# Mixture-of-experts tiles of two half tiles with an expert each, in a fused attention and expert layer

## The chip, the cores and the metric

The kernel runs on one core of a Trainium2 chip. A core has a matrix engine (PE, with its weight loads listed as PEld), a vector engine (DVE), a scalar engine (ACT), a general engine (POOL) and a queue processor (SP) that only issues transfers. Each works off its own list of instructions in order, and they wait for each other by semaphores. The metric is the device time of one execution in microseconds (us).

## The reference

For 128 sequences of 64 tokens with 128 features, the reference first adds a gated cross-attention and then a gated mixture of experts:

```
x = x + tanh(g_xattn) * xattn(ctx, layernorm(x))        # 8 heads, keys from ctx and x
n = layernorm(x)
probs = softmax(n @ Wr + br);  top 2 of 8 experts
h = relu(n @ W1[e] + b1[e])                              # 128 -> 256
y = h @ W2[e] + b2[e]                                    # 256 -> 128
x = x + tanh(g_ffn) * sum over the 2 chosen of probs[e] * y
```

All of it is in 32-bit floats. The reference computes every expert for every token; the kernel computes only the two that are chosen.

## The kernel before

The work is cut into 16 groups of 8 sequences (512 tokens). One program written out by hand runs over slots n from -15 to 179. A slot holds the attention of one sequence in three stages (scores, softmax one slot later, output two slots later) and, by n modulo 8, one of the group's jobs: turning keys, queries, projection, residual, layernorm, routing. Every engine walks through the same slots, so the slots set the order of all queues.

The experts work on chunks of 2, 3, 3, 3, 3 and 2 groups. When a chunk's last group is routed, each token's normalised row has been scattered by POOL to a buffer in HBM that is sorted by expert (`scatter_rows`, L482). `list_tiles` (DVE) then finds which 256-row tiles of that buffer are filled, and writes a table with the first row and the expert of each. The number of tiles of a chunk is a constant, the most that any routing can need: 15, 19, 19, 19, 19, 15, together 106. A tile belongs to a single expert.

`tile_slots` gives each tile a slot: none before its chunk is routed, none in slots with n modulo 8 equal to 2 until slot 136. Slots 35 to 127 hold the 72 tiles of chunks 0 to 3, beside the attention of later groups. The attention ends with slot 130; slots 131 to 164 hold the other 34 tiles (called the tail here), one after the other.

For tile i in slot n:

- SP loads the rows into `xt` four slots ahead (L404), from an address that it read from the table.
- In slot n - 1 PE transposes them (`turn_tile`, L988), ACT copies the result to `xtT` (L618), and the weights and biases of the tile's expert, 642 columns, are copied from `wall` to `wt`: by POOL for the first 72 tiles (L516), by ACT in the tail (L643), both in `fetch_weights`.
- In slot n PE makes the hidden layer (`hidden_tile`, L1004), and DVE adds the bias and clips at zero (L906).
- In slot n + 1 PE makes the output (`output_tile`, L1013), with the weights as the moving operand; DVE adds the bias (L934), SP stores it (L412).

Expert numbers and row numbers are data, so they go through registers: `values_load_multi_w_load_instructions` loads up to eight of them from the table in one instruction, and checks the bounds of each with two more. POOL and ACT do that for the expert (L512, L639), SP for the row (L400), once for 8 tiles.

When a chunk's outputs are stored, POOL gathers them for each group (`gather_rows`, L495, eight indirect transfers per group), DVE adds them to the residual (`combine`, L880 and L885), and SP writes the result. In the attention PE multiplies scores (L1024), transposes the probabilities (L1032) and multiplies them with the values (L1041); the queries (L945 to L947) and the projection (L1072) are jobs of a group.

Of the kernel before, what the change touches and what calls it, by code (L numbers as in the profile page):

```python
# [32 lines left out]
TILE = 256  # L33
J = ROWS // TILE

TILES = tuple((2 * c * TOK + E * (TILE - 1)) // TILE for c in CHUNKS)
# [6 lines left out]
PACK = 2 * D + 2 * D + 2 + D  # L43
# [18 lines left out]
AT_ONCE = 8  # L62
# [68 lines left out]
def flamingo(nc, x, ctx_in, g_xattn, g_ffn, gamma_m, beta_m, gamma_l, beta_l, Wq, bq, Wkv, bkv, Wo, bo,  # L131
# [5 lines left out]
    with ctx:  # L137
# [100 lines left out]
        wt = sb("wt", [P, WB, PACK])  # L238
        hs = sb("hs", [P, 2, 2, TILE])
# [72 lines left out]
        got_x = [sem(f"got_x{b}") for b in range(XB)]  # L312
        wt_early = sem("wt_early")
# [34 lines left out]
        def wait_tiles_read(eng, k):  # L348

            for b in range(XB):  # L350
                wait(eng, got_x[b], 16 * len(range(b, FIRST_TILE[k + 1], XB)))
# [16 lines left out]
        def _(sp):  # L368
            def weights(n):
# [11 lines left out]
                if n == 0:  # L381
                    sp.dma_start(wall[:, :, 0:2 * D], W1.rearrange("e d n -> d e n")).then_inc(got_experts, 16)
                    for c in range(2):
                        sp.dma_start(wall[:, :, (2 + c) * D:(3 + c) * D], W2[:, c * D:(c + 1) * D, :].rearrange("e p n -> p e n")).then_inc(got_experts, 16)
                        sp.dma_start(wall[:, :, 4 * D + c], b1[:, c * D:(c + 1) * D].rearrange("e p -> p e"),  # L385
                                     allow_slow_non_contiguous=True).then_inc(got_experts, 16)
                    sp.dma_start(wall[:, :, 4 * D + 2:PACK], b2.partition_broadcast(P)).then_inc(got_experts, 16)
# [3 lines left out]
            def load_tile(i):  # L391
# [5 lines left out]
                if t % AT_ONCE == 0:  # L397
                    first_rows.clear()
                    m = min(AT_ONCE, TILES[k] - t)
                    _, got = nc.values_load_multi_w_load_instructions(table[0:1, k, t:t + m], engines=(mybir.EngineType.SP,),  # L400
                                                                      min_val=0, max_val=E * ROWS - TILE)
                    first_rows.update(zip(range(i, i + m), got))
                wait(sp, xt_ready, i - XB + 1)
                sp.dma_start(xt[:, i % XB, :, :], xs[k % SETS][bass.ds(first_rows[i], TILE), :].rearrange("(a p) d -> p a d", a=2)).then_inc(got_x[i % XB], 16)  # L404
# [37 lines left out]
        def _(pool):  # L442
# [21 lines left out]
            nc.gpsimd.iota(begins[:, 0, :, :], [[ROWS, E], [TILE, J]], base=0, channel_multiplier=0,  # L464
# [36 lines left out]
            def fetch_weights(i):  # L501
# [3 lines left out]
                if i == 0:  # L505
                    pool.wait_ge(got_experts, 16 * 6)
                if t == 0:
                    wait_shared(pool, shared_out, "table", LAST_GROUP[k], 0)
                if t % AT_ONCE == 0:
                    experts.clear()  # L510
# [617 lines left out]
```

## Time and profile before

| | us |
|---|---|
| median of 3 runs | 954.1 (952.58 to 955.68) |
| the profiled execution, its own time | 955.86 |
| its span, first to last instruction | 953.8 |
| PE busy, of the span | 808.2 (85%) |
| DVE, ACT, POOL busy | 601.6, 514.6, 491.2 |
| attention ends, tail of tiles begins | about 808.7 |
| last tile's output written by DVE | 924.8 |

How to read it: a busy PE is one with a matrix multiplication in flight; a record holds the way through the array too, so busy times overlap and the distance between the starts of two records says more than their length. A 32-bit multiplication is two records. The names of engines with a q (SPq) are their instruction processors.

### The profile page before, as it was taken

Reading aid. Unit: us, or ns where it says so; the run is one execution under the profiler, and the core shown is the slowest. Engines: PE = TensorE matmul, PEld = TensorE weight load, DVE = VectorE, ACT = ScalarE, POOL = GpSimd, SP = SyncE. Lnnn points to the kernel's source line nnn. Section 1 sums busy time; section 2 is a strip of 40 time slices with the busy share of each in tenths; the row PEclk is TensorE's granted clock in tenths of the full one; section 3 lists DMA queues with packets and bytes.
Section 4 is the critical chain, followed back from the end, with each engine's and each line's share of the span. In section 5 each row is a group of like instructions: output and inputs, shape, how many; then the busy total and the mean of one; then the engine's idle time right before and its main releaser. Section 6 shows DMA issues by size and latency. Waiting matters only on the chain.

```text
span 953.8 us, 15888 instructions
## 1 busy us (share of the span) xinstructions
PE 808.2 (85%) x4481; PEld 605.4 (63%) x4481; DVE 601.6 (63%) x1908; ACT 514.6 (54%) x1655; POOL 491.2 (52%) x510
## 2 busy tenths in 40 slices
PE   4747888788999898999899999899999898777760
PEld 4534556464878674878686778677777764656650
DVE  3515475755767756878767677959686754655461
ACT  3537657475757375757475757566666553323320
POOL 2103235252636355766363676657675656572645
PEclk9979999999999999999999999999999999879995
DMA  4953233102121112232212132313131213344532
GB/s 129 372 167 144 86 130 117 50 29 56 53 78 58 52 40 78 64 95 70 74 50 73 51 95 73 89 45 106 51 90 58 81 51 94 96 126 128 139 113 63
DMA packets 113976, 86.14 MB, mean 90 GB/s; under 512 B 11985, under 2 KB 104418, under 8 KB 113890
## 3 DMA queue, kind: packets, MB, share of 16 engines
q1 hardware_dynamic: 99618, 49.32, 18.8%
q0 software_dynamic: 8192, 16.79, 6.0%
q10 hardware_dynamic: 6080, 19.02, 5.0%
q8 instruction: 37, 0.61, 0.3%
q14 instruction: 49, 0.40, 0.1%
HBM read 39.74 MB, written 45.35 MB: 89 GB/s over the span
## 4 chain that ended last, share of the span: by engine, by line
PE 69%; DVE 10%; ACT 7%; issue 5%; SPq 4%; DMA 2%; POOL 2%; POOLq 0%; ACTq 0%; DVEq 0%
PE shared L1072 12%; PE batch L1041 12%; PE batch L1024 9%; PE y_ps L1013 8%; PE hid_ps L1004 8%; PE batch L1032 4%; ACT probs L592 3%; PE shared L947 3%; PE shared L945 3%; PE shared L946 3%; PE xt_ps L988 2%; ACT pT_sb L600 2%; DVE hs L906 2%; SPq L385 2%; PE batch L1004 2%
## 5 line engine op out<-in xcount | busy, mean ns | idle before, releaser
L537 POOL TENSOR_TENSOR probs<-probs,rsums 128x512 f32<-128x512 f32 x128 | 134.6, 1051 | 291.1 <-DVE rsums L900 289.9
L612 ACT ACTIVATE oT<-batch 128x512 f32<-128x512 f32 x128 | 76.5, 598 | 209.0 <-PE shared L1072 114.5
L592 ACT ACTIVATE probs<-batch,neg_max 128x128 f32<-128x128 f32 x512 | 180.4, 374 | 11.8 <-DVE neg_max L894 11.8
L894 DVE TENSOR_REDUCE neg_max<-batch 128x4 f32<-128x512 f32 x128 | 88.0, 687 | 118.8 <-PE batch L1024 117.5
L1041 PE MATMUL batch<-pT_sb,kvn 128*128 128x512 f32 x256 | 140.5, 631 | 24.3 <-ACT pT_sb L600 24.0
L495 POOL DMA_INDIRECT yg<-sorted_y,home x128 | 126.3, 987 | 64.8 <-issue 32.6
L1024 PE MATMUL batch<-kvT,qT 128*128 128x128 f32 x1024 | 141.7, 282 | 17.4 <-ACT oT L612 17.4
L1024 PEld LDWEIGHTS batch<-kvT,qT 128*128 128x128 f32 x1024 | 129.2, 193 | 41.9 <-ACT oT L612 28.7
L482 POOL DMA_INDIRECT sorted_x<-xn,row_of x128 | 130.6, 1020 | 32.5 <-issue 32.0
L1013 PEld LDWEIGHTS y_ps<-wt,hs 128*128 128x128 f32 x848 | 110.1, 196 | 19.1 <-issue 16.3
L1013 PE MATMUL y_ps<-wt,hs 128*128 128x128 f32 x848 | 116.3, 281 | 5.9 <-DVE y_sb L934 5.9
L1072 PE MATMUL shared<-oT,M 128*128 128x512 f32 x256 | 119.3, 610 | 0.8 <-ACT oT L612 0.8
L592 ACT ACTIVATION_READ_ACCUMULATOR probs<-batch,neg_max 128x1 f32 x512 | 110.1, 215 | 0.0
L655 ACT ACTIVATE qT<-shared,tb 128x512 f32<-128x512 f32 x128 | 87.8, 688 | 30.2 <-PE shared L947 26.5
L1004 PE MATMUL hid_ps<-xtT,wt 128*128 128x256 f32 x356 | 94.2, 388 | 8.8 <-issue 8.7
L600 ACT ACTIVATE pT_sb<-batch 128x512 f32<-128x512 f32 x128 | 77.9, 609 | 37.7 <-PE batch L1032 36.3
L906 DVE TENSOR_SCALAR hs<-hid_ps,wt 128x256 f32<-128x256 f32 x178 | 77.1, 474 | 33.5 <-PE hid_ps L1004 33.3
L934 DVE TENSOR_TENSOR y_sb<-y_ps,wt 128x256 f32<-128x256 f32 x106 | 44.3, 418 | 79.3 <-PE y_ps L1013 75.4
L1032 PE MATMUL batch<-ident,probs 128*128 128x128 f32 x512 | 79.6, 279 | 13.3 <-POOL probs L537 13.3
L1072 PEld LDWEIGHTS shared<-oT,M 128*128 128x128 f32 x256 | 48.5, 199 | 51.3 <-issue 51.3
L618 ACT ACTIVATE xtT<-xt_ps 128x256 f32<-128x256 f32 x106 | 40.3, 380 | 63.6 <-PE xt_ps L988 63.6
L1004 PEld LDWEIGHTS hid_ps<-xtT,wt 128*128 128x128 f32 x356 | 61.8, 194 | 16.3 <-issue 11.5
(132 smaller groups left out, 1226.4 us busy)
## 6 DMA issues: line engine op xcount, KB each, us to landing
sorted_x<-yg ACTq DMA_DIRECT2D x36, 512.0 KB, 3.6
xt<-sorted_x SPq DMA_DIRECT2D x106, 128.0 KB
sorted_y<-y_sb SPq DMA_DIRECT2D x106, 128.0 KB
kv<-in_ctx_dram SPq DMA_DIRECT2D x16, 256.0 KB, 3.8
kv<-in_x_dram SPq DMA_DIRECT2D x16, 256.0 KB, 4.3
xres<-in_x_dram SPq DMA_DIRECT2D x16, 256.0 KB, 3.0
out_dram<-x SPq DMA_DIRECT2D x16, 256.0 KB
sorted_x<-xn,row_of POOLq DMA_INDIRECT x128, 2.3
```

The costliest lines, as they stand in the source:

```text
L482: nc.gpsimd.indirect_dma_start(xs[k % SETS][:, :], bass.IndirectOffsetOnAxis(ap=row_of[:, g, choice, c:c + 1], axis=0), xn[:, g % 2, c, :] ...
L495: nc.gpsimd.indirect_dma_start(yg[:, g % 2, c, choice, :], None, ys[k % SETS][0:TILES[k] * TILE, :], bass.IndirectOffsetOnAxis(ap=home[:, ...
L537: nc.gpsimd.tensor_tensor(pv, pv, rsums[:, m % 2, :].unsqueeze(2).broadcast_to([P, 4, P]), ALU.mult).then_inc(probs_ready, 1)
L592: last = nc.scalar.activation(probs[:, m % 2, c * P:(c + 1) * P], batch_ps[m % 3][:, c * P:(c + 1) * P], ACT.Exp, bias=neg_max[:, m % 2, c ...
L600: nc.scalar.activation(pT_sb[:, :], batch_ps[m % 3][:, :], ACT.Copy).then_inc(pT_done, 1)
L906: last = nc.vector.tensor_scalar(hs[:, i % 2, c, :], hid(i)[:, c * TILE:(c + 1) * TILE], wt[:, i % WB, 4 * D + c:4 * D + c + 1], 0.0, ALU. ...
L1004: last = nc.tensor.matmul(hid(i)[:, c * TILE:(c + 1) * TILE], wt[:, i % WB, c * D:(c + 1) * D], xtT[:, i % 2, :], start=True, stop=True)
L1013: last = nc.tensor.matmul(y_ps[:, a * D:(a + 1) * D], hs[:, i % 2, c, a * P:(a + 1) * P], wt[:, i % WB, (2 + c) * D:(3 + c) * D], start=(c ...
L1024: last = nc.tensor.matmul(batch_ps[n % 3][:, c * P:(c + 1) * P], qT[:, g % 2, b, 2 * c:2 * c + 2, :].rearrange("p h i -> p (h i)"), kvT[:, ...
L1032: last = nc.tensor.transpose(batch_ps[m % 3][:, c * P:(c + 1) * P], probs[:, m % 2, c * P:(c + 1) * P], ident[:, :])
L1041: nc.tensor.matmul(batch_ps[m % 3][:, :], kvn[:, g % 3, b, :], pT_sb[:, :], start=True, stop=True).then_inc(o_ready, 1)
L1072: last = nc.tensor.matmul(sh[:, :], M[:, h, :], oT[:, h, :], start=(h == 0), stop=(h == H - 1))
```

## The change

A tile stays 256 rows, but is now two half tiles of 128 rows, each with an expert of its own. Since padding goes only to the next 128 rows, a chunk needs at most 24 or 32 halves: 12, 16, 16, 16, 16, 12 tiles, 88 in all. Slots 35 to 124 hold 60 tiles, slots 131 to 158 the other 28. The last gather moves from slots 172 to 175 to slots 166 to 169. The table now lists halves, `J` is 12 * 8 entries instead of 6 * 8.

For each half there is one load of rows and one copy of weights. A copy is 386 columns: first-layer weights, first bias, second bias. The second-layer weights are not copied: PE reads them in `wall` at an address that it computes from the expert's register, for which PE loads the table too (`read_table` in `output_tile`). `AT_ONCE` is 4 tiles, again eight values to a load.

The hidden layer is four multiplications of 128 columns instead of two of 256. Since relu(h + b1) = max(h, -b1) + b1, DVE takes the maximum with -b1 in one instruction over 512 columns, and b1 times W2 is added to the second bias once, in slots 10 to 13 (`fold_biases`).

```diff
--- before.py
+++ after.py
@@ -30,17 +30,25 @@
-TILE = 256
-J = ROWS // TILE
-
-TILES = tuple((2 * c * TOK + E * (TILE - 1)) // TILE for c in CHUNKS)
+
+HALF = 128
+TILE = 2 * HALF
+J = ROWS // HALF
+
+HALVES = tuple((2 * c * TOK + E * (HALF - 1)) // HALF for c in CHUNKS)
+TILES = tuple((m + 1) // 2 for m in HALVES)
...
-PACK = 2 * D + 2 * D + 2 + D
+
+
+USED = 2 * D + 2 + D
+PACK = USED + 2 * D
+
+BIASES = 10
...
-AT_ONCE = 8
+AT_ONCE = 4
...
+        def read_table(engine, row, got, i, upto, biggest):
+
+            k = CHUNK_OF_TILE[i]
+            t = i - FIRST_TILE[k]
+            m = min(AT_ONCE - t % AT_ONCE, TILES[k] - t, upto - i)
+            _, values = nc.values_load_multi_w_load_instructions(table[row:row + 1, k, 2 * t:2 * (t + m)], engines=(engine,),
+                                                                 min_val=0, max_val=biggest)
+            got.clear()
+            got.update({(i + h // 2, h % 2): value for h, value in enumerate(values)})
...
-                sp.dma_start(xt[:, i % XB, :, :], xs[k % SETS][bass.ds(first_rows[i], TILE), :].rearrange("(a p) d -> p a d", a=2)).then_inc(got_x[i % XB], 16)
+                for a in range(2):
+                    sp.dma_start(xt[:, i % XB, a, :], xs[k % SETS][bass.ds(first_rows[i, a], HALF), :]).then_inc(got_x[i % XB], 16)
...
-                nc.gpsimd.tensor_copy(wt[:, i % WB, :], wall[:, bass.ds(experts[i], 1), :].rearrange("p e n -> p (e n)")).then_inc(wt_early, 1)
+                for a in range(2):
+                    last = nc.gpsimd.tensor_copy(wt[:, i % WB, a, :], wall[:, bass.ds(experts[i, a], 1), 0:USED].rearrange("p e n -> p (e n)"))
+                last.then_inc(wt_early, 1)
...
-                nc.scalar.activation(wt[:, i % WB, :], wall[:, bass.ds(experts[i], 1), :].rearrange("p e n -> p (e n)"),
-                                     ACT.Copy).then_inc(wt_late, 1)
+                for a in range(2):
+                    last = nc.scalar.activation(wt[:, i % WB, a, :], wall[:, bass.ds(experts[i, a], 1), 0:USED].rearrange("p e n -> p (e n)"),
+                                                ACT.Copy)
+                last.then_inc(wt_late, 1)
...
+            def fold_biases(n):
+
+                for half in range(2):
+                    mine = slice(4 * half, 4 * half + 4)
+                    if n == BIASES + 2 * half:
+                        dve.wait_ge(got_experts, 16 * 6)
+                        nc.vector.tensor_copy(hs[:, :, :, :, :].rearrange("p t a c j -> p (t a) c j"),
+                                              wall[:, mine, 2 * D:2 * D + 2].unsqueeze(3).broadcast_to([P, 4, 2, HALF])).then_inc(b1_wide, 1)
+                    if n == BIASES + 2 * half + 1:
+                        dve.wait_ge(b2_folded, half + 1)
+                        bias = wall[:, mine, 2 * D + 2:USED]
+                        nc.vector.tensor_tensor(bias, (hid_ps, y_ps)[half][:, :].rearrange("p (e n) -> p e n", e=4), bias,
+                                                ALU.add).then_inc(b1_wide, 1)
+                if n == BIASES + 3:
+                    dve.wait_ge(b1_wide, 4)
+                    nc.vector.tensor_scalar(wall[:, :, 2 * D:2 * D + 2], wall[:, :, 2 * D:2 * D + 2], -1.0, None, ALU.mult).then_inc(experts_ready, 1)
...
-                    for c in range(2):
-                        last = nc.vector.tensor_scalar(hs[:, i % 2, c, :], hid(i)[:, c * TILE:(c + 1) * TILE],
-                                                       wt[:, i % WB, 4 * D + c:4 * D + c + 1], 0.0, ALU.add, ALU.max)
-                    last.then_inc(hs_done, 1)
+                    nc.vector.tensor_tensor(hs[:, i % 2, :, :, :], hid(i)[:, :].rearrange("p (a c j) -> p a c j", a=2, c=2),
+                                            wt[:, i % WB, :, 2 * D:2 * D + 2].unsqueeze(3).broadcast_to([P, 2, 2, HALF]),
+                                            ALU.max).then_inc(hs_done, 1)
...
+            def fold_biases(n):
+                for half in range(2):
+                    if n == BIASES + 2 * half + 1:
+                        pe.wait_ge(b1_wide, 2 * half + 1)
+                        for e in range(4):
+                            for c in range(2):
+                                last = nc.tensor.matmul((hid_ps, y_ps)[half][:, e * D:(e + 1) * D], hs[:, e // 2, e % 2, c, :],
+                                                        wall[:, 4 * half + e, USED + c * D:USED + (c + 1) * D],
+                                                        start=(c == 0), stop=(c == 1))
+                        last.then_inc(b2_folded, 1)
...
-                for c in range(2):
-                    last = nc.tensor.matmul(hid(i)[:, c * TILE:(c + 1) * TILE], wt[:, i % WB, c * D:(c + 1) * D], xtT[:, i % 2, :],
-                                            start=True, stop=True)
+                for a in range(2):
+                    for c in range(2):
+                        last = nc.tensor.matmul(hid(i)[:, (2 * a + c) * HALF:(2 * a + c + 1) * HALF], wt[:, i % WB, a, c * D:(c + 1) * D],
+                                                xtT[:, i % 2, a * HALF:(a + 1) * HALF], start=True, stop=True)
                 last.then_inc(hid_ready, 1)
 
             def output_tile(i):
+                k = CHUNK_OF_TILE[i]
+                t = i - FIRST_TILE[k]
+                if t == 0:
+                    wait_shared(pe, shared_out, "table", LAST_GROUP[k], 0)
+                if t % AT_ONCE == 0:
+                    read_table(mybir.EngineType.PE, 1, experts, i, N_TILES, E - 1)
                 pe.wait_ge(hs_done, i + 1)
                 wait(pe, y_done, i)
                 for a in range(2):
                     for c in range(2):
-                        last = nc.tensor.matmul(y_ps[:, a * D:(a + 1) * D], hs[:, i % 2, c, a * P:(a + 1) * P],
-                                                wt[:, i % WB, (2 + c) * D:(3 + c) * D], start=(c == 0), stop=(c == 1))
+                        last = nc.tensor.matmul(y_ps[:, a * D:(a + 1) * D], hs[:, i % 2, a, c, :],
+                                                wall[:, bass.ds(experts[i, a], 1), USED + c * D:USED + (c + 1) * D].rearrange("p e n -> p (e n)"),
+                                                start=(c == 0), stop=(c == 1))
                 last.then_inc(y_ready, 1)
...
```

PE in an attention slot with a query job (n modulo 8 is 4), at the first tile of a chunk, before: `batch` holds a sequence's scores, `shared` the query, `y_ps` the tile's output.

```order
L1041 MATMUL batch1<-pT_sb,kvn 128x512
L988 MATMUL xt_ps<-ident,xt 128x128 x2
L945 MATMUL shared1<-latT_hi,A_hi 128x512
L946 MATMUL shared1<-latT_lo,A_hi 128x512
L947 MATMUL shared1<-latT_hi,A_lo 128x512
L1013 MATMUL y_ps<-wt,hs 128x128 x4
```

PE at the same kind of place after, where t % 4 is 0:

```order
L1093 MATMUL batch1<-pT_sb,kvn 128x512
L1019 MATMUL xt_ps<-ident,xt 128x128 x2
L976 MATMUL shared1<-latT_hi,A_hi 128x512
L977 MATMUL shared1<-latT_lo,A_hi 128x512
L978 MATMUL shared1<-latT_hi,A_lo 128x512
L381 TENSOR_LOAD table
L381 ISA x16
L1064 ISA
L1064 MATMUL y_ps<-wall,hs 128x128
L1064 ISA
L1064 MATMUL y_ps<-wall,hs 128x128
```

The load of eight registers and 16 instructions on them now stand between the query and the output, and one register instruction before each of the output's four multiplications. There are 22 such loads on PE, and 352 such multiplications.

ACT in the tail at a read of the table, before: `xtT` is the transposed tile, `wt` its weights.

```order
L618 ACTIVATE xtT<-xt_ps 128x256
L639 TENSOR_LOAD table
L639 ISA x16
L643 ISA
L643 ACTIVATE wt<-wall 128x642
L618 ACTIVATE xtT<-xt_ps 128x256
```

ACT in the tail at a read of the table, after:

```order
L634 ACTIVATE xtT<-xt_ps 128x256
L381 TENSOR_LOAD table
L381 ISA x16
L656 ISA
L656 ACTIVATE wt<-wall 128x386
L656 ISA
L656 ACTIVATE wt<-wall 128x386
```

The single copy has become two. Such a read stands in the tail seven times now (five times before, two of them with fewer than eight values).

PE in the tail, two slots later than that read of ACT, before:

```order
L1004 MATMUL batch0<-xtT,wt 128x256 x2
L988 MATMUL xt_ps<-ident,xt 128x128 x2
L1013 MATMUL y_ps<-wt,hs 128x128 x4
L1004 MATMUL hid_ps<-xtT,wt 128x256 x2
L988 MATMUL xt_ps<-ident,xt 128x128 x2
```

PE in the tail, after:

```order
L1049 MATMUL batch0<-xtT,wt 128x128 x4
L1019 MATMUL xt_ps<-ident,xt 128x128 x2
L381 TENSOR_LOAD table
L381 ISA x16
L1064 ISA
L1064 MATMUL y_ps<-wall,hs 128x128
```

The read stands between the transposition of the next tile and the output of the tile before.

## Rows read from the trace of the kernel before

**Rows 1.** The page: PE's busy time, and its granted clock in 40 slices.

```profile
PE 808.2 (85%) x4481; PEld 605.4 (63%) x4481; DVE 601.6 (63%) x1908; ACT 514.6 (54%) x1655; POOL 491.2 (52%) x510
PEclk9979999999999999999999999999999999879995
```

**Rows 2.** Windows: stretch, length, busy (instructions) of PE, PEld, DVE, ACT, POOL; clock.

```profile
493.99:510.72 16.73, 16.45 (x103) 13.12 (x102) 12.86 (x45) 11.66 (x39) 8.21 (x9) 1.00 0.17 51
349.68:363.61 13.93, 11.16 (x63) 8.12 (x63) 10.01 (x35) 10.34 (x37) 11.06 (x10) 1.00 0.19 57
```

**Rows 3.** Timeline of PE in two attention slots: start, length, line, operation.

```profile
494.23 1.12 PE L1041 MATMUL batch<-pT_sb,kvn 128*128 128x512 f32 x2
496.11 1.05 PE L1013 MATMUL y_ps<-wt,hs 128*128 128x128 f32 x8
...
552.26 1.11 PE L1041 MATMUL batch<-pT_sb,kvn 128*128 128x512 f32 x2
553.43 1.06 PE L1013 MATMUL y_ps<-wt,hs 128*128 128x128 f32 x8
```

**Rows 4.** Timeline of POOL around its second read of the table.

```profile
286.07 1.03 POOL L537 TENSOR_TENSOR probs<-probs,rsums 128x512 f32<-128x512 f32 x1 [6.10 <-DVE rsums L900]
288.86 0.72 POOL L516 COPY wt<-wall 128x642 f32 x1 [1.76 <-issue]
```

**Rows 5.** Timeline of ACT in the tail.

```profile
862.52 0.38 ACT L618 ACTIVATE xtT<-xt_ps 128x256 f32<-128x256 f32 x1 [1.46 <-PE xt_ps L988]
862.80 0.73 ACT L643 ACTIVATE wt<-wall 128x642 f32 x1
864.99 0.38 ACT L618 ACTIVATE xtT<-xt_ps 128x256 f32<-128x256 f32 x1 [1.46 <-PE xt_ps L988]
...
873.71 0.38 ACT L618 ACTIVATE xtT<-xt_ps 128x256 f32<-128x256 f32 x1 [1.46 <-PE xt_ps L988]
...
876.21 0.74 ACT L643 ACTIVATE wt<-wall 128x642 f32 x1 [2.12 <-issue]
```

**Rows 6.** Chain of waits in the tail: start, length, what; "issue" is PE held back.

```profile
808.66 3.66 issue
...
863.38 0.25 issue
...
865.84 1.57 issue
...
874.56 2.48 issue
...
901.32 1.22 issue
```

**Rows 7.** Groups by line: busy us, mean ns of one, idle before.

```profile
L643 ACT ACTIVATE wt<-wall 128x642 f32 x34 | 24.9, 734 | 12.4 <-issue 6.5 <-DVE y_sb L934 6.0
L563 ACT ACTIVATE probs<-xt_ps 128x384 f32<-128x384 f32 x4 | 2.0, 490 | 1.6 <-PE xt_ps L954 1.1 <-issue 0.5
L906 DVE TENSOR_SCALAR hs<-hid_ps,wt 128x256 f32<-128x256 f32 x178 | 77.1, 474 | 33.5 <-PE hid_ps L1004 33.3
```

**Rows 8.** Groups by line: two steps of `list_tiles`, 48 and 96 columns wide.

```profile
L849 DVE SCALAR_TENSOR_TENSOR hit<-key,tile_id,begins 128x96 f32<-128x96 f32 x6 | 1.9, 318 | 0.2
L843 DVE TENSOR_TENSOR key<-nth,start_tile 128x48 f32<-128x48 f32 x6 | 1.2, 207 | 0.2
```

**Rows 9.** Windows in the tail, as in rows 2.

```profile
850.00:876.00 26.00, 20.26 (x130) 17.19 (x128) 15.46 (x43) 9.19 (x18) 12.50 (x13) 1.00 0.51 143
876.00:883.00 7.00, 5.84 (x28) 5.18 (x28) 3.17 (x10) 2.71 (x5) 0.00 (x0) 0.76 0.39 111
```

**Rows 10.** Timeline of PE after the longest of those gaps.

```profile
877.05 1.10 PE L1004 MATMUL batch<-xtT,wt 128*128 128x256 f32 x4 [2.48 <-issue]
...
880.06 1.72 PE L1004 MATMUL hid_ps<-xtT,wt 128*128 128x256 f32 x4
```

**Rows 11.** Chain of waits at the end.

```profile
924.38 0.42 DVE y_sb L934
```

More of the change, by code:

```diff
@@ L350, in wait_tiles_read @@
             for b in range(XB):
-                wait(eng, got_x[b], 16 * len(range(b, FIRST_TILE[k + 1], XB)))
+                wait(eng, got_x[b], 32 * len(range(b, FIRST_TILE[k + 1], XB)))
         def wait_rows_scattered(eng, k):
@@ L397, in load_tile @@
                 if t % AT_ONCE == 0:
[L398 to L402, printed above, removed]
+                    read_table(mybir.EngineType.SP, 0, first_rows, i, N_TILES, E * ROWS - HALF)
                 wait(sp, xt_ready, i - XB + 1)
-                sp.dma_start(xt[:, i % XB, :, :], xs[k % SETS][bass.ds(first_rows[i], TILE), :].rearrange("(a p) d -> p a d", a=2)).then_inc(got_x[i % XB], 16)
+                for a in range(2):
+                    sp.dma_start(xt[:, i % XB, a, :], xs[k % SETS][bass.ds(first_rows[i, a], HALF), :]).then_inc(got_x[i % XB], 16)
             def store_tile(i):
@@ L509, in fetch_weights @@
                 if t % AT_ONCE == 0:
-                    experts.clear()
-                    m = min(AT_ONCE, TILES[k] - t, LATE - i)
-                    _, got = nc.values_load_multi_w_load_instructions(table[1:2, k, t:t + m], engines=(mybir.EngineType.Pool,),
-                                                                      min_val=0, max_val=E - 1)
-                    experts.update(zip(range(i, i + m), got))
+                    read_table(mybir.EngineType.Pool, 1, experts, i, LATE, E - 1)
                 wait(pool, y_done, i - WB + 1)
-                nc.gpsimd.tensor_copy(wt[:, i % WB, :], wall[:, bass.ds(experts[i], 1), :].rearrange("p e n -> p (e n)")).then_inc(wt_early, 1)
+                for a in range(2):
+                    last = nc.gpsimd.tensor_copy(wt[:, i % WB, a, :], wall[:, bass.ds(experts[i, a], 1), 0:USED].rearrange("p e n -> p (e n)"))
+                last.then_inc(wt_early, 1)
             for n in range(FIRST, LAST + 1):
@@ L853, in list_tiles @@
                     nc.vector.tensor_reduce(found[:, :], hit[:, :, :], AX, ALU.add).then_inc(table_step, 1)
-                    nc.vector.tensor_scalar(gap[:, :], n_tiles[:, 0:E - 1], -float(TILE), float(ROWS), ALU.mult, ALU.add).then_inc(table_step, 1)
+                    nc.vector.tensor_scalar(gap[:, :], n_tiles[:, 0:E - 1], -float(HALF), float(ROWS), ALU.mult, ALU.add).then_inc(table_step, 1)
                     m = 8 * CHUNKS[k]
@@ L927, in slot @@
                 keep_table(n, s)
+                fold_biases(n)
                 if n in COMBINE_AT:
```

31 lines of the change are left out of this document (16 added, 15 removed).

## The prediction

> **What bounds the kernel now.** I read the page first. PE is busy for 85% of the span, no other engine above 63%, and the granted clock stays near full until the last eighth, where it dips [rows 1]. So PE and what holds it back set the time, and the tail is a place of its own. Then the windows over slots of the attention. Slots 77 to 79, with a tile each, take 16.73 us, and PE is busy for 16.45 of them. Slots 53 to 55 do the same jobs of a group without tiles in 13.93 us, with PE busy for 11.16 [rows 2]. With tiles the attention is bound by PE, without them by the chain between the engines; so a tile costs (16.73 - 13.93) / 3 = 0.93 us, though it is 2.0 us of work on PE: an output is eight records in 1.06 us, of which the last one's way through the array is no work, so 0.11 us each and 0.9 together [rows 3]; a hidden layer has as many columns, a transposition takes 0.2.
>
> In the tail the chain of waits puts a small "issue" of 0.25 us ahead of a hidden layer [rows 6], and the timeline of ACT says why: from one `xtT` to the next it is 864.99 - 862.52 = 2.47 us, and the copy of the weights starts 0.28 us after `xtT` and runs for 0.73 [rows 5]. PE with its 2.0 us waits for ACT's copy. The loop is transposition, `xtT`, copy, hidden layer. The reads of the table stand out: an ordinary copy follows `xtT` by 0.28 us, the one behind a read of eight values by 876.21 - 873.71 = 2.50 [rows 5], so a read costs the loop 2.2 us, and PE shows a gap of 2.48 [rows 6]. The last tile's output is written at 924.8, and 29 us of gathering and writing follow that the change leaves as they are [rows 11].
>
> **The change, part by part.** All sums are against the profiled execution (955.86 us, of which 953.8 are the span); it was 1.8 us above the median of 954.1, to which I add the differences.
>
> *Twelve tiles fewer in the attention.* 12 x 0.93 = 11.2 us gained. The lower end is 8 (slots where the list of tiles is made wait for DVE anyway), the upper is PE's whole work, 24.
>
> *PE reads the table, 15 times in the attention.* No row of before shows PE doing this. The nearest are ACT's read (2.50 us from `xtT` to the copy) and POOL's, 288.86 - 286.07 = 2.79 us for seven values, of which only the 1.03 us of the multiplication ahead hide a part [rows 4, 5]. I take 2.5. The read is work of PE's sequencer, so it lies beside what the array has still to do. But the sequencer gets past the multiplication L1041 only when ACT has released it, and from there to the output it is 553.43 - 552.26 = 1.17 us, or 496.11 - 494.23 = 1.88 with a query between [rows 3]. Beyond that cover PE stands still for 1.3 or 0.6 us, in slots in which it is already full. By `tile_slots` the reads fall on n modulo 8 of 4 (four times) and 5 (four times), both with a query, 0 (four times), and 1 (three times, where the list of tiles is waited for; I take 1 us for the three). 8 x 0.6 + 4 x 1.3 + 1 = 11 us lost. Ends: 0 (all covered) and 15 x 2.5 = 38. Queued behind the read are the output and the next scores, for which DVE and ACT wait, so little of this is given back.
>
> *Register work for each output multiplication.* 352 times. A read is one load and 16 register instructions in 2.5 us, so one costs at most 0.15 us; a pair of records of 128 columns keeps the array for 2 x 0.11. I take 0, hidden beside the array; if the array waited for each, 352 x 0.1 = 35 us.
>
> *Hidden layer in four pieces.* Eight records instead of four, for the same columns. 0.02 us for each of 60 tiles, 1 us; in the tail nothing.
>
> *Folding the biases, slots 10 to 13.* 16 multiplications, 32 records x 0.11 = 3.5 us of PE's work, in slots without tiles, where (as above) about half of such work shows; DVE's four instructions of 512 or 1024 columns stand ahead of its next maximum. 2 us, ends 0 and 6.
>
> *The list over 96 entries instead of 48.* The step with 96 columns takes 318 ns, one with 48 takes 207 [rows 8]. Some six steps get 0.06 to 0.2 us longer, 0.5 us for each chunk; PE waits for the result. 2 us, ends 0 and 4.
>
> *POOL.* 15 reads of eight instead of 11, and two copies of 386 for one of 642. POOL has slack on average, but not where scatters and a read meet. 1 us, ends 0 and 6. SP issues two loads per tile, four slots ahead: 0. DVE's first instruction gets shorter (two of 474 ns [rows 7] become one), but nobody waits for it: 0.
>
> Attention: -11.2 + 11 + 1 + 2 + 2 + 1 = +6.
>
> *Tail, six tiles fewer:* 6 x 2.47 = 14.8 us gained.
>
> *Two copies on ACT.* 642 columns take 734 ns; 384 columns take 490 [rows 7], so two halves are 2 x 0.49, less the 0.1 by which a second instruction overlaps the first (`xtT` runs 0.38, the copy starts after 0.28 [rows 5]). 0.88 - 0.73 gives 0.15, with the second address some 0.2 us, and it is in the loop: 28 x 0.2 = 5.6 lost. Ends 0 and 0.35 per tile (10).
>
> *ACT's reads.* Seven of eight values: 7 x 2.2 = 15.4. Before there were five; their gaps between 808.66 and 901.32 sum to 10.6 [rows 6], less the ordinary 0.25 each 9.3, since one read has only three values (1.57) and others fall where PE is late anyway. 6 lost.
>
> *PE's reads in the tail.* Seven. After the transposition is issued the sequencer reads for 2.5 us; the output of 0.9 us comes behind, and the next hidden layer behind that. From hidden layer to hidden layer that is 0.15 + 2.5 + 0.9 = 3.55 instead of 2.47 + 0.2. 7 x 0.9 = 6 lost; ends 0 and 7 x 2.5 = 17.
>
> *The clock.* The stretch before the gap of 2.48 us has a clock of 1.00, the one behind it 0.76 [rows 9], which is a mean of the two levels; the hidden layer at 880.06 takes 1.72 us instead of 1.10, and comes 3.01 us behind the one before instead of 2.47 [rows 10]. Before, about four such stretches of two tiles cost 1.1 us each; after, seven, with two gaps in each block of four tiles, at 1.3 to 1.7 each. 5 lost, ends 0 and 20. The Trainium skill, page "TensorE: Matmul & The Clock Gate", section "HAM oscillation — how this bites in real kernels", says that a loop whose bursts are shorter than its waits drops to the lower clock in every round. By that rule the tail would fall back in each of its blocks; it is the third rival below. The trace agrees as far as it goes: one long gap, one drop.
>
> Tail: -14.8 + 5.6 + 6 + 6 + 5 = +8. Together +14 to +15: 954.1 + 14.9 = 969.
>
> **The rivals.**
>
> *PE's reads are hidden.* If the sequencer is far enough ahead of the array, they cost nothing, and the gaps that they open in the tail don't come: 969 - 11 - 6 - 4 = 948. This ends on the other side. For it: a read needs nothing of the array, and DVE or ACT would have to be the ones that are late. It decides where the array has more than 2.5 us of work queued at a read. Against it: 1.17 and 1.88 us of cover [rows 3]. The Trainium skill, "PSUM — Partial Sum Buffer", section "Engine vs sequencer instructions", speaks for it: the sequencer waits only until earlier instructions are dispatched, not until they are complete. No row of PE here shows such an instruction. By that rule the read still has only the cover of the work that is already queued, so it does not change my sum.
>
> *Work of PE counts in full.* 12 x 2.0 and 6 x 2.47 = 39 gained, less 16 for the parts in the attention and on ACT: 931. Against it: the windows, where a tile is worth 0.93.
>
> *The clock stays low in the tail.* At half clock a tile is 4.0 us of PE's work instead of a loop of 2.67. For half of 28 tiles that is 14 x 1.3 = 18, of which 5 are counted: 982. For it: two gaps within four tiles. Against it: the clock was full again after two tiles [rows 9].
>
> *Register addresses hold the array up*, 35 us: 1004. Nothing in the trace shows it; ACT and POOL do the same kind of instruction ahead of each copy, with no gap that shows (0.28 us is less than `xtT` takes) [rows 5].
>
> **How the numbers follow.** Forecast 0.50 (its own range 957 to 981), reads hidden 0.20, PE's work in full 0.06, low clock 0.14, register addresses 0.07, the rest near no change. The range from 945 to 988 leaves out the second and fourth rivals and little more. A difference of 0.3% is about what this kernel's runs can tell from none. Faster: the first two rivals and a bit of the forecast's edge, 0.25. Within 0.3%: 0.07. Slower: 0.68.
>
> **What would show it.** In slots 77 to 79, now free, about 14 us. In PE's rows at the first, fifth, ninth and thirteenth tile of a chunk, a gap labelled issue of 1 us or more ahead of the output in slots with n modulo 8 of 0, half of it in 4 and 5; with no gap there, the first rival is right. In the tail 2.6 to 2.8 us from one `xtT` to the next instead of 2.47; every fourth tile 4.8 on ACT's account, and 3.5 two slots later on PE's. The tail from the attention's end to the last output takes 116 us before; I expect 122 to 128. If it takes under 110, the loop over ACT was not the bound. Clocks below 0.8 in more windows than four. If the eight records of an output stand further apart than 0.11 us, the register addresses do cost.

## The result, and the profile after

The changed kernel takes 988.9 us (median of 4: 985.25 to 995.3), the kernel before 954.4 beside it: 1.037 times as long, interval 1.031 to 1.043. Forecast were 969 and at most 988. It is slower, as forecast, but by 34.5 us instead of 14.9. The profiled execution took 985.25 us, its span is 983.5.

The page after. First PE and its clock, which answer to [rows 1]; then groups by line (busy us, mean ns | idle before):

```profile
PE 795.1 (81%) x4613; PEld 605.2 (62%) x4613; DVE 580.9 (59%) x1771; ACT 510.1 (52%) x1659; POOL 498.5 (51%) x558
...
PEclk9779999899999999999999999999999899779895
...
L1064 PE MATMUL y_ps<-wall,hs 128*128 x704 | 102.8, 293 | 40.1 <-issue 36.9
...
L1049 PE MATMUL hid_ps<-xtT,wt 128*128 128x128 f32 x592 | 84.6, 290 | 20.7 <-issue 20.7
...
L531 POOL COPY wt<-wall 128x386 f32 x120 | 62.3, 545 | 24.9 <-issue 24.9
```

PE is busy for 13 us less, in a span that is 30 us longer. The idle time stands ahead of the output multiplication (L1064), under "issue": no other engine is named. The clock dips once more in the tail, for longer.

The timeline of PE in slot 64, where the output follows the placement of rows (L1140, L1142), with the row of DVE that the placement waits for, and then the view of the table's readers at that place (PEldq is PE's instruction processor):

```profile
416.27 1.02 PE L1093 MATMUL batch<-pT_sb,kvn 128*128 128x512 f32 x2
416.70 0.39 DVE L830 TENSOR_SCALAR chosen<-rank 128x32 bf16<-128x32 f32 x1
417.13 0.38 PE L1019 MATMUL xt_ps<-ident,xt 128*128 128x128 f32 x2
417.35 0.18 PE L1140 MATMUL shared<-chosen,earlier 128*128 128x40 bf16 x1
417.38 0.24 PE L1142 MATMUL shared<-chosen,every 128*128 128x32 bf16 x4
420.54 1.15 PE L1064 MATMUL y_ps<-wall,hs 128*128 x8 [2.92 <-issue]
```

```profile
L381 PEldq TENSOR_LOAD <-table x1: 587/587/587, 417.3 to 417.3; - x1
```

The load of eight values takes 0.59 us and ends at 417.85, but the output starts at 420.54. In the trace's records of PE's instruction processor, the time between holds a register operation (0.15 us) and a range assertion (0.02) for each value, one pair every 0.28 us, eight times. From the start of the load to the output's first record it is 3.28 us here, and 3.16 to 3.45 (median 3.2) over the 22 reads. On ACT and POOL a pair comes every 0.22 to 0.23 us, on SP every 0.25 to 0.26. The read began only at 417.26, because the placement ahead of it had waited for DVE's `chosen`, done at 417.09. The work queued on PE then ended at 417.62, 0.36 us after the read began: the 1.17 us of cover in [rows 3] weren't there. Over all 22 reads the idle time before the output sums to 39.4 us: 25.9 in the 15 of the attention, 13.5 in the 7 of the tail.

The tail, on the timeline (ACT and PE; compare [rows 5]) and in windows (columns as in [rows 2]):

```profile
889.84 0.38 ACT L634 ACTIVATE xtT<-xt_ps 128x256 f32<-128x256 f32 x1 [1.48 <-PE xt_ps L1019]
892.32 0.94 ACT L656 ACTIVATE wt<-wall 128x386 f32 x2 [2.10 <-issue]
...
893.36 2.04 PE L1049 MATMUL hid_ps<-xtT,wt 128*128 128x128 f32 x8 [2.66 <-issue]
...
895.87 0.38 ACT L634 ACTIVATE xtT<-xt_ps 128x256 f32<-128x256 f32 x1 [2.61 <-PE xt_ps L1019]
...
898.56 0.38 ACT L634 ACTIVATE xtT<-xt_ps 128x256 f32<-128x256 f32 x1 [1.48 <-PE xt_ps L1019]
...
900.65 1.15 PE L1064 MATMUL y_ps<-wall,hs 128*128 x8 [2.13 <-issue]
```

```profile
890.70:893.30 2.60, 0.00 (x0) 0.00 (x0) 0.42 (x1) 0.94 (x2) 1.34 (x2) 0.98 0.55 156
893.30:897.20 3.90, 3.81 (x19) 3.68 (x19) 0.71 (x2) 1.21 (x3) 0.00 (x0) 0.58 0.12 34
897.20:900.65 3.45, 1.32 (x10) 1.09 (x11) 1.10 (x2) 1.21 (x3) 0.00 (x0) 1.00 0.22 62
900.65:904.30 3.65, 3.20 (x27) 3.04 (x27) 1.54 (x3) 1.21 (x3) 0.00 (x0) 1.00 0.24 68
```

A block of four tiles has both gaps: 2.66 behind ACT's read, 2.13 behind PE's own. After the first the clock is mostly at the lower of its levels (0.58 of full) and the hidden layer takes 2.04 us instead of 1.13. Undisturbed, one `xtT` follows the other by 898.56 - 895.87 = 2.69 us, as forecast (2.67). Behind ACT's read it is 895.87 - 889.84 = 6.03 us and not the 4.8 forecast, because the hidden layer and the transposition in between ran at the lower clock. From hidden layer to hidden layer across PE's read it is 901.64 - 897.17 = 4.47 instead of 3.55. The clock fell behind the gap of 2.66 and not behind the one of 2.13 (1.00). The rule in the Trainium skill, "TensorE: Matmul & The Clock Gate", section "HAM oscillation — how this bites in real kernels", is about a loop whose bursts of work are shorter than its waits. Between these two gaps PE works for 5.2 us, longer than either gap. So the rule doesn't say that the clock falls in each block; the prediction had read it that way.

Slots 77 to 79 answer to [rows 2]. They aren't quite without tiles: the output of the tile of slot 76 stands in slot 77, as the timeline shows. The second window takes in slot 80 too.

```profile
504.65 1.05 PE L1064 MATMUL y_ps<-wall,hs 128*128 x8
```

```profile
502.75:517.51 14.76, 12.07 (x71) 9.02 (x71) 10.26 (x36) 10.28 (x36) 9.01 (x8) 1.00 0.22 63
502.75:521.56 18.81, 15.33 (x94) 11.38 (x94) 14.13 (x46) 13.31 (x47) 11.99 (x12) 1.00 0.20 58
```

The same four slots of the kernel before:

```profile
493.99:514.84 20.85, 20.02 (x134) 16.16 (x132) 16.90 (x56) 14.53 (x50) 9.26 (x9) 1.00 0.18 54
```

### The profile page after: what moved, and what is told of

The parts are those of the page before. It is cut to its first block, busy times and chain, and to the rows that moved or that the text cites. A ratio compares the mean times of both kernels' runs of the same rounds, so it can differ in the third digit from the quotient of the medians.

```text
span 983.5 us, 17233 instructions
## 1 busy us (share of the span) xinstructions
PE 795.1 (81%) x4613; PEld 605.2 (62%) x4613; DVE 580.9 (59%) x1771; ACT 510.1 (52%) x1659; POOL 498.5 (51%) x558
## 4 chain that ended last, share of the span: by engine, by line
PE 66%; issue 9%; ACT 9%; DVE 8%; SPq 4%; POOL 2%; DMA 2%; ACTq 0%; POOLq 0%; DVEq 0%
PE shared L1125 12%; PE batch L1093 11%; PE batch L1076 9%; PE y_ps L1064 8%; PE hid_ps L1049 7%; PE batch L1084 4%; ACT probs L608 4%; PE shared L978 3%; PE shared L976 3%; PE shared L977 3%; ACT pT_sb L616 2%; PE xt_ps L1019 2%; PE batch L1049 2%; ACT oT L628 2%; SPq L406 1%
## 5 line engine op out<-in xcount | busy, mean ns | idle before, releaser
L1076 PEld LDWEIGHTS batch<-kvT,qT 128*128 128x128 f32 x1024 | 132.5, 198 | 50.5 <-ACT oT L628 34.0
L1076 PE MATMUL batch<-kvT,qT 128*128 128x128 f32 x1024 | 146.1, 288 | 21.5 <-ACT oT L628 21.5
L1064 PE MATMUL y_ps<-wall,hs 128*128 x704 | 102.8, 293 | 40.1 <-issue 36.9
L1064 PEld LDWEIGHTS y_ps<-wall,hs 128*128 128x128 f32 x704 | 95.7, 206 | 56.4 <-issue 54.7
L1049 PE MATMUL hid_ps<-xtT,wt 128*128 128x128 f32 x592 | 84.6, 290 | 20.7 <-issue 20.7
L965 DVE TENSOR_TENSOR y_sb<-y_ps,wt 128x256 f32<-128x256 f32 x88 | 37.1, 421 | 94.9 <-PE y_ps L1064 94.7
L1049 PEld LDWEIGHTS hid_ps<-xtT,wt 128*128 128x128 f32 x592 | 77.1, 204 | 23.3 <-issue 23.3
L936 DVE TENSOR_TENSOR hs<-hid_ps,wt 128x512 f32<-128x512 f32 x74 | 51.0, 689 | 43.4 <-PE hid_ps L1049 43.0
L531 POOL COPY wt<-wall 128x386 f32 x120 | 62.3, 545 | 24.9 <-issue 24.9
```

The costliest lines, as they stand in the source:

```text
L1049: last = nc.tensor.matmul(hid(i)[:, (2 * a + c) * HALF:(2 * a + c + 1) * HALF], wt[:, i % WB, a, c * D:(c + 1) * D], xtT[:, i % 2, a * HAL ...
L1064: last = nc.tensor.matmul(y_ps[:, a * D:(a + 1) * D], hs[:, i % 2, a, c, :], wall[:, bass.ds(experts[i, a], 1), USED + c * D:USED + (c + 1 ...
L1076: last = nc.tensor.matmul(batch_ps[n % 3][:, c * P:(c + 1) * P], qT[:, g % 2, b, 2 * c:2 * c + 2, :].rearrange("p h i -> p (h i)"), kvT[:, ...
```

## The experiments

"After" is the changed kernel. The runs are from four chips, and the kernel before ran beside each of them, so kernels are compared by their ratio to it; the bracket is its 95% interval. The runs e1 to e7 and e9 are from two chips where the kernel before takes 952 to 955 us (11 and 5); e8 and e10 to e15 are from two where it takes 1005 to 1007 (12 and 1), so there only ratios count. The diffs are shortened.

**PE's reads without checks, all reads without checks, no reads, fixed addresses.**

```diff
 # e1: for PE alone; e2: for all engines
-    engines=(engine,), min_val=0, max_val=biggest)
+    engines=(engine,), min_val=0, max_val=biggest, skip_runtime_bounds_check_because="...")
 # e3: no read by PE; e3 and e4: weights at a fixed place
-    wall[:, bass.ds(experts[i, a], 1), USED + c * D:...]
+    wall[:, a, USED + c * D:...]
```

> The changed kernel with one thing altered: TensorE's read of the table is issued without the two bound instructions behind each of its eight values, so a read is the load (0.59 us) and little else instead of 3.2 us. Theory A (the reads' bound work on TensorE is the loss): the idle time labelled issue before the output matmuls falls from about 39 us (26 in the attention, 13 in the tail) to under 8, attention gives back about 20 and the tail about 11: 989 -> 955 to 962. Rival B (TensorE's register addresses on the 352 output matmuls cost it): idle time shrinks but the time stays above 975. Rival C (the waits for GpSimd's and ScalarE's reads set the slots, TensorE's idle time lies beside them): 980 to 989.

> As the run before, and the reads of SyncE, GpSimd and ScalarE also without bound instructions (eight values each, 1.9 us on ScalarE and GpSimd in the traces so far, about 0.55 left). Theory A: a further 5 to 12 us, since ScalarE's read in the tail (14 values of idle time at five reads) and GpSimd's at the slots that grew (62, 86, 95, 110, 119) go too: 945 to 955, which may be below the kernel before. Rival C: the larger part of the fall comes here, not in the run before: this one 15 us or more below it. If neither matters: 985 to 990.

> TensorE reads no table and takes second weights of experts 0 and 1 for the two halves of every tile, at fixed addresses (it leaves out the choice of the second layer's weights by expert; all else is computed). Theory A: the same as the unbounded read minus its load of 0.6 us, 22 times, of which part is hidden: 945 to 955, 2 to 10 below the first run. Rival B (register addresses cost): 20 or more below the first run. Rival C: 980 to 989.

> TensorE still reads the table as in the changed kernel, bounds and all, but the output matmuls take fixed addresses (it leaves out the choice of the second layer's weights by expert). Theory A: addresses cost nothing, the time is that of the changed kernel, 984 to 992. Rival B (register addresses hold the array): 10 us or more below it. Rival C: 980 to 989 as well, told apart by the other runs.

e3 and e4 leave out the choice of the second layer's weights by expert. Measured: e1 954.2 us (ratio 1.0009, 0.998 to 1.004), e2 928.5 (0.974, 0.970 to 0.978), e3 954.9 (1.002, 1.000 to 1.005), e4 984.5 (1.033, 1.029 to 1.037). e1 alone gives back all that the change had lost; e3, without reads or register addresses, is no better. So neither the load nor the addresses cost anything that these runs can tell from none (e4 is 0.4% below after, inside the intervals), and the checks of PE's reads cost 35 us. The rival of the register addresses falls twice: e3 is not faster than e1, and e4's interval overlaps that of after. e2 fell by a further 26 us, far more than the 5 to 12 expected; the rival named there had 15 or more, though the larger part stays with PE. The same place in e1, PE's timeline, and the page's line:

```profile
412.19 0.24 PE L1143 MATMUL shared<-chosen,every 128*128 128x32 bf16 x4
412.97 1.15 PE L1065 MATMUL y_ps<-wall,hs 128*128 x8 [0.54 <-issue]
```

```profile
L1065 PE MATMUL y_ps<-wall,hs 128*128 x704 | 96.9, 282 | 2.6 <-DVE y_sb L966 1.4
```

The idle 40.1 has become 2.6; at slot 64 the load alone leaves 0.54. What e2 takes away besides is seen on POOL. First e1, then e2, in slot 95 and the start of the next:

```profile
601.62 1.04 POOL L554 TENSOR_TENSOR probs<-probs,rsums 128x512 f32<-128x512 f32 x1 [1.30 <-DVE rsums L932]
604.38 0.95 POOL L532 COPY wt<-wall 128x386 f32 x2 [1.73 <-issue]
605.49 1.01 POOL L514 DMA_INDIRECT yg<-sorted_y,home  x1 [0.16 <-issue]
608.09 0.95 POOL L514 DMA_INDIRECT yg<-sorted_y,home  x1 [1.58 <-issue]
609.06 1.05 POOL L554 TENSOR_TENSOR probs<-probs,rsums 128x512 f32<-128x512 f32 x1
```

```profile
597.12 1.04 POOL L554 TENSOR_TENSOR probs<-probs,rsums 128x512 f32<-128x512 f32 x1 [0.64 <-DVE rsums L932]
598.10 0.95 POOL L532 COPY wt<-wall 128x386 f32 x2
599.21 1.02 POOL L514 DMA_INDIRECT yg<-sorted_y,home  x1 [0.15 <-issue]
601.71 0.96 POOL L514 DMA_INDIRECT yg<-sorted_y,home  x1 [1.48 <-issue]
602.69 1.05 POOL L554 TENSOR_TENSOR probs<-probs,rsums 128x512 f32<-128x512 f32 x1
```

With the read, POOL goes from one multiplication of the probabilities to the next without waiting for another engine, in 7.44 us; it is the bound of that slot. Without checks it takes 5.57. And in e2's tail, with most of the gaps gone, the clock stays up (window as above; in after 0.77 for the same stretch, in e1 0.89, in before 0.91):

```profile
840.00:900.00 60.00, 44.28 (x350) 40.35 (x349) 30.25 (x72) 22.91 (x56) 33.63 (x36) 0.97 0.52 144
```

**The suspected costs put on the kernel before.**

```diff
 # e5: PE, ahead of every fourth tile's output; the values are not used
+    if t % 4 == 0:
+        m = 2 * min(4, TILES[k] - t)
+        nc.values_load_multi_w_load_instructions(table[1:2, k, t:t + m], engines=(PE,), min_val=0, max_val=E - 1)
 # e6 and e13: all reads of the kernel before
+    skip_runtime_bounds_check_because="..."
```

> The kernel before, plus 28 reads of eight values by TensorE ahead of every fourth tile's output matmuls, with bounds, whose values nobody uses. Theory A (the read itself costs): in the changed kernel 22 reads left 39.4 us of idle time, 1.79 each; 28 of them give +50: 995 to 1010, and the kernel before at 1.045 to 1.06. Rival B (what costs is the reads together with the two halves, three matmul shapes and more waits): less than +20, below 975. Rival C (slots are set by other engines): below 960.

> The kernel before with the reads of SyncE, GpSimd and ScalarE without bound instructions: 16 reads by each list, eight values each. In the changed kernel this took 26 us beside TensorE's. Half as many values are read here, and the tail's copy of 642 columns takes ScalarE 0.73 us with ScalarE setting the tail's pace as in the changed kernel: theory A gives -8 to -14, 939 to 946, so that the fair price of the 18 tiles gone is 1 to 2 per cent. Rival (the gain from unbounded reads belongs to the kernel before just as much): 928 or less, and the halves are worth nothing.

> The kernel before with unbounded reads, a second time, now beside the two below on one chip: 0.989 of the kernel before.

Measured: e5 989.1 us, ratio 1.039 (1.032 to 1.046), just below the 1.045 expected. The idle time before its outputs at the reads is 39.7 us for 28 of them, 1.4 each and not 1.79. Six of the 28 are of six values only (three tiles are left there), which the expectation overlooked, and behind the placement the gap is 1.5 to 1.6 in the attention, where after has up to 2.92. Still, reads alone make the kernel before as slow as after. e6 took 943.9 (0.989, 0.984 to 0.995) and e13 0.988 (0.984 to 0.992), as expected: the kernel before too loses 11 us to checks.

**The other corner, and other places for the read.**

```diff
 # e8: checks only on PE's reads
 # e9: PE's read moved from ahead of the output to ahead of pe.wait_ge(probs_ready, ...)
 # e12: PE reads at each tile
-    if t % AT_ONCE == 0: read_table(PE, 1, experts, i, N_TILES, E - 1)
+    read_table(PE, 1, experts, i, N_TILES, E - 1, at_once=1)
```

> The changed kernel with the reads of SyncE, GpSimd and ScalarE without bounds and TensorE's with them: the fourth corner beside the changed kernel (989), TensorE's alone unbounded (954) and all unbounded (928.5). If the two costs add: 989 - 26 = 963. If in the tail they lie on one cycle and each hides a part of the other: 968 to 975. If TensorE's read covered the others': 955 to 960.

> The changed kernel with TensorE's read, bounds and all, moved from just ahead of the output matmuls to just behind the scores of the same slot, ahead of the wait for the probabilities. Theory A: TensorE's sequencer stands 3.2 us there instead, and the array has the scores' four matmuls (about 0.9 us) and then a wait for the probabilities that mostly lasts longer: the read hides in the attention (up to -20), in the tail it has nothing ahead of it and costs as much as before or a little more: 965 to 978. Rival (the place doesn't matter, the array is kept busy to the last in every slot): 985 to 992.

> The changed kernel with TensorE reading the two values of one tile ahead of each tile's output matmuls, bounds and all, instead of eight values ahead of every fourth: the same 176 values and 66 loads more. Theory A (a read costs what of it outlasts the array's queued work: 0.6 + 2 x 0.28 = 1.15 us a read against 1.2 to 1.9 us of queued work in most slots and 0.2 behind the placement's wait): nearly all hidden, idle time issue before the output matmuls from 39 us to 5 to 15, 955 to 968. Rival (the array pays for each value read, wherever: 176 x 0.28 = 49 us, and for each load): 989 or more, up to 1030.

Measured: e8 1.008 (1.005 to 1.012), or 962 where the kernel before takes 954: the two costs add. e12 1.002 (0.998 to 1.006), or 956: with all its checks, PE's read cut into pieces of two values costs nearly nothing. Its page has less than half the idle time before the outputs (40.1 in after):

```profile
L1063 PE MATMUL y_ps<-wall,hs 128*128 x704 | 105.6, 297 | 19.3 <-issue 12.1
```

Of the 19.3 us 4.6 are put down to waits for `y_sb`, which leaves 14.7, within the 5 to 15 expected. In the attention alone it is 5.6 us instead of 25.9. So the price is what of one read outlasts the queued work, and not the sum of the reads, which is larger in e12. e9 took 968.7 (1.015, 1.009 to 1.021), in the expected range but not for the expected reason. The attention (here from the first to the last multiplication of probabilities on POOL) won 6.9 us instead of up to 20, the tail behind it 10.0 instead of nothing, the start 1.8. Why the tail won is open. PE in slot 60 of e9 shows why in the attention:

```profile
386.37 1.05 PE L1072 MATMUL batch<-kvT,qT 128*128 128x128 f32 x8
388.57 0.65 PE L1088 MATMUL batch<-ident,probs 128*128 128x128 f32 x4 [1.15 <-issue]
```

The gap is labelled issue and not a wait for POOL: the read stands in the way here too, and no wait is there to hide it (POOL had finished the probabilities at 384.60).

**Weights copied, and the biases alone.**

```diff
 # e7: second-layer weights copied with the first's, no read by PE
-    wt = sb("wt", [P, WB, 2, USED])
+    wt = sb("wt", [P, WB, 2, PACK])
 # e11: the kernel before with fold_biases and the maximum
-    tensor_scalar(hs[:, i % 2, c, :], hid(i)[...], wt[...], 0.0, ALU.add, ALU.max)   # twice
+    tensor_tensor(hs[:, i % 2, :, :], hid(i)[...], wt[...].broadcast_to(...), ALU.max)
```

> The changed kernel with the second layer's weights copied with the first's (two copies of 642 columns per tile instead of 386) and no read by TensorE. Theory A: TensorE's 39 us go, and the longer copies cost GpSimd 0.3 to 0.4 us a half in 60 early tiles, partly hidden, and ScalarE 0.25 to 0.3 us a half in the tail's 28 tiles, +15 where ScalarE sets the pace: 960 to 975. Rival (the copies were the loss, reads by TensorE beside them harmless): above 989.

> The kernel before with one part of the change alone: the second bias folded once at the start, the first bias as a maximum, one instruction of VectorE instead of two. The folding lengthened two slots near the start by 1.17 us each in the trace of the changed kernel (+2.3), and 106 maxima at 0.69 stand against pairs of 0.64: +2 to +5, 956 to 959; nothing (953 to 955) if the start is hidden in its noise of about 2 us.

Measured: e7 980.6 us (1.027, 1.022 to 1.033), above the 975 expected: taking PE's reads out by longer copies gives back 8 of the 35 us. e11 0.998 (0.995 to 1.001): no price of the biases can be told from none, though two slots near the start are 1.15 to 1.17 us longer each (6.34 instead of 5.19 and 5.17), as in after.

**A version that beats both.**

```diff
 # e10 and e15: e2, and in the tail ScalarE copies the weights ahead of xtT
+    if n >= B and TILE_AT.get(n + 1, 0) >= LATE: fetch_weights(TILE_AT[n + 1])
     act.wait_ge(xt_ready, i + 1)
     nc.scalar.activation(xtT[:, i % 2, :], xt_ps[:, 0:TILE], ACT.Copy)
```

> All reads unbounded (928.5), and in the tail (tiles after the last batch) ScalarE copies a tile's first-layer weights ahead of its copy of xtT instead of behind it. In the trace a tail tile takes 2.79: transposes, then the copy of xtT 0.39 after an idle 1.48, two weight copies 0.93, and TensorE idle 0.45 before the hidden matmuls. With the weight copies in the idle time the hidden matmuls start up to 0.9 earlier and TensorE's own 2.57 per tile is the bound: about 0.2 a tile over 26 tiles, 922 to 925. Rival (the copies wait for a free weight buffer, so xtT comes later): 930 to 940.

> The changed kernel with all reads unbounded, beside the run above: if the 18 tiles gone are worth 15 us of 944 (as two separate calls gave), 0.974 of the kernel before and 0.984 of the run above. If a difference between calls made that, the two lie within 0.5 per cent.

> The run above with ScalarE's weight copies ahead of its copy of xtT in the tail: 0.2 to 0.3 us a tile for 26 tiles, 0.006 to 0.008 below the run above, 0.966 of the kernel before. If another chip made that difference, within 0.3 per cent of the run above.

Measured: e14 0.973 (0.967 to 0.980); e10 0.966 (0.960 to 0.972) and e15 0.965 (0.960 to 0.971). The ratios of e2 and e6 come back on a slower chip, so the halved tiles without checks are worth 1.5% (0.973 / 0.988 = 0.985). The new order gains about 0.8% more; the intervals of e14 and e15 overlap, but all four executions of e15 (968.2 to 973.5) lie below all four of e14 (974.8 to 983.7), which ran beside them. Its mechanism shows in ACT of e15:

```profile
920.40 0.94 ACT L659 ACTIVATE wt<-wall 128x386 f32 x2 [1.28 <-DVE y_sb L968]
921.25 0.37 ACT L637 ACTIVATE xtT<-xt_ps 128x256 f32<-128x256 f32 x1
922.41 0.94 ACT L659 ACTIVATE wt<-wall 128x386 f32 x2 [0.80 <-DVE y_sb L968]
923.26 0.37 ACT L637 ACTIVATE xtT<-xt_ps 128x256 f32<-128x256 f32 x1
```

From one `xtT` to the next it is 2.01 us here instead of 2.69, and the copy now waits for a free buffer (`y_sb` done). The expectation had PE's 2.57 as the floor; that was wrong, since it added up overlapping record lengths.

## Why the prediction was partly right and partly wrong

Its sum can be split by differences of the spans, one profiled execution each, where the kernel before takes 952 to 955 us. "Attention" runs from the 21st multiplication of probabilities on POOL, before the first tile, to the last. The start is counted up to the 21st, because what the kernels differ by at the first one (40.8 to 43.5) is made up by then:

| | before | e6 | after | e1 | e2 |
|---|---|---|---|---|---|
| start | 159.0 | 157.3 | 158.4 | 158.5 | 158.4 |
| attention | 638.0 | 638.7 | 659.7 | 643.0 | 635.9 |
| tail | 156.8 | 143.7 | 165.4 | 150.8 | 132.1 |

The starts alone differ by up to 1.7, and after's attention is 2.8 above e4's, so a term is good to 2 or 3 us.

- **PE's reads, after minus e1** (forecast 11 and 6): attention 16.7, tail 14.6; 31 of the span and 35 of the median. This is the step that failed. "I take 2.5" was 3.2 from the load to the output, a size borrowed from ACT and POOL. "Beyond that cover PE stands still for 1.3 or 0.6 us" measured 1.25 to 1.52 at n modulo 8 of 4 and 5, where the cover was 1.9 us as forecast and only the read's size was wrong. At 0 it was 1.65 to 2.92, since the cover was only 0.4 to 1.6 where jobs of a group wait for DVE ahead of the read (the placement in slot 64). At 1 it was 1.7 to 2.0, not 1 us for the three together. That makes 25.9 us of idle time in the attention against the forecast's 11.
- **"So little of this is given back"** failed too, the other way: e1 has 25.3 us less of this idle time in the attention, but the attention is only 16.7 us shorter, so a third came back. At 4, 5 and 0 the six slots around a read are 1.2 to 3.4 us longer in after than in e1, in most within half a microsecond of the gap; but around the reads in slots 73 and 97 (n modulo 8 of 1) they are 1.7 and 3.3 us shorter. e5 says the same: 24.5 us idle, 18.4 us longer than before. That the sequencer is the place and that only what outlasts queued work counts, e1, e5 and e12 showed.
- **The tail's 14.6** hold the clock's part: with the same multiplications PE is busy there for 92.6 us in after and 84.4 in e1, and idle for 72.8 and 66.4. So 8 of the 14.6 are longer busy time, at a mean clock of 0.79 against 0.83, and 6 are standing still; the forecast had 5 and 6.
- **The other engines' reads, (e1 - e2) - (before - e6)** (forecast POOL 1, ACT 6): attention 7.1 + 0.7 = 7.8, tail 18.7 - 13.1 = 5.6. ACT's term fits. POOL's was given the low end "since it has slack on average"; the text had named where a scatter and a read meet, and in slots such as the 95th POOL is the bound. This is the second term that was mis-sized, at or above its upper end of 6. SP's reads are in these differences too, and no run takes them apart.
- **The rest, e2 - e6** (forecast attention -11.2 + 3 and start + 2, tail -14.8 + 10.6): -2.8, +1.1 and -11.6. In the attention a tile gone was worth 0.68 us instead of 0.93: the three tiles gone shorten slots 77 to 80 from 20.85 to 18.81 us, and as much from e6 to e2. The forecast's "14 us" for slots 77 to 79 took them as free, but an output stands in the first. Twelve tiles at 0.68 instead of 0.93 are 3 of the missing 5.4; the rest is open. In the tail -14.8 + 5.6 without the clock's 5 would be -9.2, so the clock's term belongs to the reads, and 2.4 are open.
- **Sum**: attention 16.7 + 7.8 - 2.8 = +21.7 against +4, start -0.6 against +2; tail 14.6 + 5.6 - 11.6 = +8.6 against +8. The tail was right only by luck, because two errors cancelled. The forecast's own terms, +6 and +8, make 14 and not the 14.9 that it added.
- **Biases +2**: as forecast in two slots, but made up before the 21st multiplication, and not measurable as a whole (e11). **Register addresses 0**: right (e3, e4); records of an output still stand 0.11 us apart. **Two copies on ACT**: right, 2.69 from `xtT` to `xtT`. **Hidden layer in four pieces, list of 96**: not tried by themselves.
- **Rivals.** "Reads are hidden" falls by the 39.4 us of idle time. By the Trainium skill, "PSUM — Partial Sum Buffer", section "Engine vs sequencer instructions", the sequencer waits for dispatch alone. The rows of slot 64 agree, since the load began at 417.26 and L1142 ran from 417.38 to 417.62, and they show how little that helped. "Work of PE counts in full" is refuted by e2. "Low clock" came true in part: 0.77 from 830 to 890 against 0.89 in before. It is 0.89 in e1 and 0.97 in e2 over the same stretch, so it follows the gaps. The range missed by 1 us: it reached 19 above the forecast, though the ends of PE's reads alone (38 and 17 against 11 and 6) reached 38 above.

## What to carry to other kernels

A read of a table into registers costs its engine the load and, per value, the checks; look for it as idle time "issue" ahead of the instruction behind it. On the busiest engine cut it into pieces shorter than the work that is surely queued there, or leave checks out where the program bounds the values itself (then nothing stops a wrong one). Take the cover from the slot with the latest wait, not from a typical one, measure a read on the engine that will do it, and price a term by its own two ends before calling it slack. Idle time in front of one instruction isn't yet time lost: here a third of it came back in the attention.

## What was not expected of the hardware

- Checks, not loads, make a read dear: 0.28 us per value on PE, 0.22 to 0.26 elsewhere, against 0.59 for the load of eight. PE's load agrees with the floor of about 600 ns for such an instruction in the Trainium skill, "DMA: Bandwidth & Descriptors", section "Latency and other measured facts".
- Matrix multiplications whose moving operand has a register address ran as fast as those with a fixed one, within what e3 and e4 can tell (e3 1.002 against e1 1.001, e4 1.033 against 1.037).
- On chip 1, one of the two slower ones, e14, the same kernel as e2, needed 976.1 us of span instead of 926.5. The attention took 5 us longer; nearly all else is in the tail, with a clock of 0.69 to 0.78 from 830 to 920 and a few long gaps. The chain of waits in e14 has one, and ACT's timeline the row behind it:

```profile
823.85 0.89 PE y_ps L1065 x8
824.74 11.94 issue
```

```profile
834.94 0.39 ACT L635 ACTIVATE xtT<-xt_ps 128x256 f32<-128x256 f32 x1 [13.39 <-remote]
```

PE had ended the transposition that this copy reads at 823.85, so PE waited for ACT, and ACT for something that the trace doesn't name. The median time from issue to landing of the 512 KB stores that clear the sorted buffer was 8.6 us there and 4.0 in e2. Whether slower transfers make these gaps was not tried, and no row ties them to one. The ratios agree on the faster and the slower chips, for e2 and e14 (0.974, 0.973) and for e6 and e13 (0.989, 0.988).
